# A graph network on one core: left-over edges between two parts of the scatters, nodes settled block by block, row parts split beside the first group

## What is computed

```python
h = relu(layernorm(x)) @ W                       # attention
score = h[src] @ a_src + h[dst] @ a_dst
e = exp(-leaky_relu(score)) * edge_weight
rowsum = segment_sum(e, src); h_prime = segment_sum(e * h[dst], src)
h_prime = where(rowsum == 0, h, h_prime) / where(rowsum == 0, 1, rowsum)
x = x + elu(h_prime)
...
y = relu(layernorm(x))                           # three layers
for i in range(3):
    aggr = segment_sum(relu(y[src] + edge_attr), dst)
    t = relu(bn((y + aggr) @ W1[i] + b1[i]))
    y = bn(t @ W2[i] + b2[i])                    # relu but for the last
out = x + y
```

## Time and profile before

| | us |
|---|---|
| median of 3 runs | 6582.67 |
| their range | 6578.78 to 6588.45 |
| the profiled execution | 6598.86 |
| its span, first to last instruction | 6597.1 |

### The profile page before, as it was taken

The page is one execution under the profiler, slowest core; times in us unless marked ns, Lnnn a source line. Parts: engine busy times, 40 slices in busy tenths (PEclk is TensorE's granted clock), DMA queues, the critical chain, the costliest instruction groups (busy, mean ns, idle before and its releaser), DMA issues.

```text
span 6597.1 us, 140067 instructions
## 1 busy us (share of the span) xinstructions
PE 4538.8 (69%) x50455; PEld 4306.8 (65%) x50456; DVE 3977.1 (60%) x7380; ACT 2704.7 (41%) x6857; POOL 3284.4 (50%) x2579
## 2 busy tenths in 40 slices
PE   1256561001018999999388888868888887888887
PEld 1256561000008999999388888858888876888886
DVE  6378781000005666666777777767777767777776
ACT  1398991000005777777333333343333334333333
POOL 0488887777770000000355665436666635656562
PEclk6576775555558999999699999989999998999998
DMA  9955543333323444453576777647777765777774
GB/s 169 265 170 166 185 136 137 115 111 112 109 92 121 150 150 150 150 150 127 152 224 223 224 227 223 211 150 227 235 232 232 233 188 181 229 226 226 225 232 134
DMA packets 664852, 1187.18 MB, mean 180 GB/s; under 512 B 151546, under 2 KB 489292, under 8 KB 664540
## 3 DMA queue, kind: packets, MB, share of 16 engines
q1 hardware_dynamic: 447020, 836.60, 40.4%
q10 hardware_dynamic: 135824, 178.67, 8.9%
q0 software_dynamic: 81696, 167.48, 8.3%
HBM read 967.99 MB, written 214.44 MB: 179 GB/s over the span
## 4 chain that ended last, share of the span: by engine, by line
PE 59%; issue 21%; DVE 10%; another core or an unknown queue 5%; SPq 3%; DMA 1%; ACT 1%; DVEq 1%; POOL 0%; POOLq 0%; ACTq 0%
PE ps L1569 18%; PE ps L1555 13%; PE ps L1488 10%; PE ps L1475 8%; PE ps L1579 4%; PE ps L1437 2%; PE ps L1438 2%; DVE dst_hot L1262 2%; PE ps L1427 2%; DVE sums L1270 1%; SPq L474 1%; DVE unit_attr L1289 1%; DVE field L1008 1%; PE ps L1613 1%
## 5 line engine op out<-in xcount | busy, mean ns | idle before, releaser
L665 POOL DMA_INDIRECT unit_x<-gin_rows,unit_src x1449 | 1854.8, 1280 | 1369.0 <-DVE unit_attr L1289 784.4
L1569 PE MATMUL ps<-dst_hot,sums 128*128 128x128 f32 x10584 | 1610.4, 292 | 175.8 <-issue 84.5
L632 POOL DMA_INDIRECT attr_by_slot<-abuf,ridx x1080 | 1397.7, 1294 | 514.9 <-issue 335.9
L836 ACT ACTIVATE sums<-sums 128x512 f32<-128x512 f32 x1512 | 837.6, 573 | 1842.1 <-DVE sums L1270 1370.9
L1569 PEld LDWEIGHTS ps<-dst_hot,sums 128*128 128x128 f32 x10584 | 1373.1, 199 | 233.5 <-issue 135.5
L1555 PE MATMUL ps<-x_parts,src_turned 128*128 128x128 bf16 x15876 | 1225.7, 225 | 230.2 <-issue 157.1
L1270 DVE TENSOR_TENSOR sums<-ps,sums 128x512 f32<-128x512 f32 x1512 | 911.5, 619 | 777.3 <-PE ps L1555 449.1
L1555 PEld LDWEIGHTS ps<-x_parts,src_turned 128*128 128x128 bf16 x15876 | 1074.8, 102 | 281.1 <-issue 259.9
L1475 PE MATMUL ps<-h_win,turned_hot 128*128 128x130 bf16 x7791 | 603.8, 221 | 446.1 <-issue 292.3
L1262 DVE TENSOR_TENSOR dst_hot<-iota_one,dl_slot 128x896 f32<-128x896 f32 x756 | 819.2, 1084 | 0.0
L1475 PEld LDWEIGHTS ps<-h_win,turned_hot 128*128 128x128 bf16 x7791 | 506.8, 97 | 467.6 <-issue 459.4
(11 more groups left out here) (229 smaller groups left out, 4743.4 us busy)
## 6 DMA issues: line engine op xcount, KB each, us to landing
sums<-attr_by_slot SPq DMA_DIRECT2D x756, 448.0 KB
src_turned<-rows_by_group SPq DMA_DIRECT2D x756, 224.0 KB
turned_hot<-rows_by_block ACTq DMA_DIRECT2D x392, 384.0 KB
attr_by_slot<-zeros SPq DMA_DIRECT2D x36, 3136.0 KB, 25.4
unit_attr<-in_edge_attr SPq DMA_DIRECT2D x204, 448.0 KB
abuf<-in_edge_attr SPq DMA_DIRECT2D x72, 960.0 KB
unit_x<-gin_rows,unit_src POOLq DMA_INDIRECT x1449
attr_by_slot<-abuf,ridx POOLq DMA_INDIRECT x1080
```

What stands on the lines that cost most here:

```text
L632: pool.indirect_dma_start(out=attr_table, out_offset=bass.IndirectOffsetOnAxis(ap=ridx[:, g, t0 + t:t0 + t + 1], axis=0), in_=abuf[:, k % ...
L665: pool.indirect_dma_start(out=unit_x[:, k % 2, t, :], out_offset=None, in_=gin_rows[n], in_offset=bass.IndirectOffsetOnAxis(ap=unit_src[:, ...
L836: act.activation(attr[:, first:first + tiles, :], attr[:, first:first + tiles, :], ACT.Relu).then_inc(s_msg, 1)
L1569: ins = pe.matmul(ps[:, 7, 0:WINDOW], attr[:, b, :], dst_hot[:, c % HOTS, b % G_TILES, :], start=(b == 0), stop=(b == BLOCKS - 1))
```

## The change

- **Scatters in two parts.** SyncE loads halves 2 to 33, then the left-over step's columns, then halves 34 to 71. GpSimd scatters 34 halves (510 transfers), gathers the left-over rows of attention, and scatters 38 halves (570). The left-over step takes one tile at a time instead of three (`STEP = 1`).
- **Attention in two loops.** Blocks 1 and 2 are a loop; then the sums of blocks 2 to 48 are cleared, the left-over step adds to them, and blocks 3 to 47 are a second loop, block 48 behind it. In the second loop a block's sums are added to what is there instead of copied.
- **Settling beside attention.** Block b - 3 is settled in the 9 chunks of block b, 11 VectorE instructions, one exp on ScalarE at chunk 5 and a load of the block's own rows there; the last three are settled behind attention. Normalisation goes in chunks of four blocks, even ones on ScalarE, odd ones on VectorE.
- **Row parts.** Only the first two chunks stand ahead of the layer's first gather; the others are formed beside the first group's halves, and the third part of every chunk on GpSimd (in `unit_x`, so the units begin two slots later, `LATE = 2`, and GpSimd's unit gathers wait for the seven subtractions). ScalarE's round 0 is written out and no longer in the loop.
- **A layer's left-over step** stands in the last round, ahead of half 11, with its own buffers and bank 6. SyncE loads for it behind half 17, GpSimd gathers behind unit slot 1. The next layer's first loads no longer wait for it.

Its core (lines left out at "..."):

```diff
-SPLIT_AT = CHUNKS // 2 * BY_CHUNK
-HALVES = ((0, SPLIT_AT), (SPLIT_AT, BLOCKS))
+TAIL_BLOCKS = 3
+SETTLE = 9
+PART_LEAD = 2
+ELU_AT = 5
+TAIL_FROM = BLOCKS - TAIL_BLOCKS
+OWN_LOADS = BLOCKS - TAIL_BLOCKS + 1
...
+LATE = 2
...
-STEP = 3
+FAR_LOADED = 16 * (6 + 1 + REST_U + 2 + T - 1 - TAIL_T)
+
+STEP = 1
+LEFT_AT = 3
+LOADS_THEN = 34
+LAST_LEFT = BY_UNIT + KEEP_AT + 1
...
-            for k in range(2, len(loads)):
+            for k in range(2, LOADS_THEN):
...
-            sp.wait_ge(s_kept, BLOCKS)
-            sp.dma_start(own[:, :, :], h_rows.rearrange("(b p) c -> p b c", p=P)).then_inc(s_out, 16)
-            store_rows(gin_rows[0], s_normed[1], 0, s_gin_row[0])
+            for k in range(LOADS_THEN, len(loads)):
+                load_half(k)
+            store_rows(gin_rows[0], lambda c: normed(sp, c), s_gin_row)
...
+                load_halves(n, ROUNDS - 1, 0, G_HALVES + 4)
                 load_left(((gidx[:, 0, :], left_src), (gidx[:, 1, :], left_dst), (gidx[:, 2, :], left_eid), (gsm[:, 0, :], left_v)),
                           s_lg[n]["loaded"], s_lg[n]["done"])
+                load_halves(n, ROUNDS - 1, G_HALVES + 4, R_HALVES)
                 if n + 1 < LAYERS:
 
-                    sp.wait_ge(s_summed, n + 1)
...
-            for k in range(len(loads)):
+            for k in range(LOADS_THEN):
...
-            pool.wait_ge(s_elu, 4)
+            for k in range(LOADS_THEN, len(loads)):
+                scatter_half(k)
+
             for n in range(LAYERS):
-                pool.wait_ge(s_gin_row[n], 16 * CHUNKS)
+                for c in range(G_CHUNKS):
+
+                    of = slice(c * G_TILES, (c + 1) * G_TILES)
+                    pool.wait_ge(s_part, 2 * (G_CHUNKS * n + c) + 2)
+                    pool.tensor_tensor(x_parts[:, 2, of, :], unit_x[:, c % 2, :, :], x_parts[:, 1, of, :], ALU.subtract).then_inc(s_last, 1)
+                pool.wait_ge(s_last, G_CHUNKS * (n + 1))
+                pool.wait_ge(s_gin_row, 16 * CHUNKS * (n + 1))
...
+                        if i == ROUNDS - 1 and k == 1:
+                            gather_left(((gx, gin_rows[n], gidx[:, 0, :]), (gy, edge_attr, gidx[:, 2, :])), s_lg[n]["loaded"], 4, s_lg[n]["gathered"])
...
-            with act.Fori(1, BLOCKS - 1) as b:
+            with act.Fori(1, LEFT_AT) as b:
                 for c in range(A_CHUNKS):
                     weigh(b, c, True)
-            for c in range(A_CHUNKS):
-                weigh(BLOCKS - 1, c, False)
...
+            def settle(p, more):
+                act.wait_ge(s_elu, p + 2)
+                act.activation(elu[:, 0, :], sums[:, p * SUM:p * SUM + D] if isinstance(p, int) else sums[:, bass.ds(p * SUM, D)], ACT.Exp).then_inc(s_expm, 1)
+                if more:
+                    load_own(p + 1)
+
+            act.wait_ge(s_elu, 1)
+            load_own(0)
+            with act.Fori(LEFT_AT, BLOCKS - 1) as b:
+                for c in range(A_CHUNKS):
+                    weigh(b, c, True)
+                    if c == ELU_AT:
+                        settle(b - LEFT_AT, True)
+            for c in range(A_CHUNKS):
+                weigh(BLOCKS - 1, c, False)
+                if c == ELU_AT:
+                    settle(BLOCKS - 1 - LEFT_AT, False)
+                    act.dma_start(own[:, :, :], h_rows[TAIL_FROM * P:COLS, 0:D].rearrange("(b p) c -> p b c", p=P)).then_inc(s_out, 16)
...
+                first_part(0)
+                for c in range(PART_LEAD):
+                    if n == 0:
+                        for t in range(c * CHUNKS // PART_LEAD, (c + 1) * CHUNKS // PART_LEAD):
+                            keep_columns(t)
+                    second_part(c)
+                    first_part(c + 1)
...
-                vec.tensor_copy(to, ps[:, 6, 0:SUM]).then_inc(s_kept, 1)
+                if onto:
+                    vec.tensor_tensor(to, to, ps[:, 6, 0:SUM], ALU.add).then_inc(s_kept, 1)
+                else:
+                    vec.tensor_copy(to, ps[:, 6, 0:SUM]).then_inc(s_kept, 1)
...
+                if c == 0:
+                    vec.wait_ge(s_kept, p + LEFT_AT)
+                    vec.tensor_scalar(col(stat[:, 0, :]), total, 0.0, None, ALU.is_equal).then_inc(s_settled, 1)
+                    vec.scalar_tensor_tensor(col(stat[:, 1, :]), total, 0.0, total, ALU.is_equal, ALU.add).then_inc(s_settled, 1)
+                elif c == 1:
+                    vec.wait_ge(s_settled, done + 2)
+                    vec.reciprocal(col(stat[:, 3, :]), col(stat[:, 1, :])).then_inc(s_settled, 1)
+                elif c == 2:
+                    vec.wait_ge(s_settled, done + 3)
+                    vec.scalar_tensor_tensor(col(stat[:, 2, :]), total, 0.0, col(stat[:, 3, :]), ALU.not_equal, ALU.mult).then_inc(s_settled, 1)
+                elif c == 3:
+                    vec.wait_ge(s_settled, done + 4)
+                    vec.tensor_scalar(rows, rows, col(stat[:, 2, :]), None, ALU.mult).then_inc(s_settled, 1)
...
+                    vec.scalar_tensor_tensor(rows, own[:, 0, :], col(stat[:, 0, :]), rows, ALU.mult, ALU.add).then_inc(s_elu, 1)
+                elif c == ELU_AT:
+                    vec.wait_ge(s_elu, p + 2)
+                    vec.scalar_tensor_tensor(node, rows, 0.0, node, ALU.max, ALU.add).then_inc(s_settled, 1)
+                elif c == 6:
+                    vec.wait_ge(s_expm, p + 1)
+                    vec.tensor_scalar(elu[:, 0, :], elu[:, 0, :], 1.0, -1.0, ALU.min, ALU.add).then_inc(s_settled, 1)
+                elif c == 7:
+                    vec.wait_ge(s_settled, done + 7)
+                    vec.tensor_tensor(node, node, elu[:, 0, :], ALU.add).then_inc(s_settled, 1)
+                else:
+                    one = slice(p, p + 1) if isinstance(p, int) else bass.ds(p, 1)
+                    vec.wait_ge(s_settled, done + 8)
+                    vec.bn_stats(ln[:, one, :].rearrange("p o s -> p (o s)"), node).then_inc(s_settled, 1)
...
-                        keep_block(b - 1)
+                        keep_block(b - 1, onto)
+                    if onto:
+                        settle(b - LEFT_AT, c)
...
-            with vec.Fori(1, BLOCKS - 1) as b:
+            with vec.Fori(1, LEFT_AT) as b:
                 block_of(b, True)
-            block_of(BLOCKS - 1, False)
-            keep_block(BLOCKS - 1)
+            link(vec.memset(sums[:, (LEFT_AT - 1) * SUM:BLOCKS * SUM], 0.0))
...
+            vec.sem_inc(s_elu, 1)
+            with vec.Fori(LEFT_AT, BLOCKS - 1) as b:
+                block_of(b, True, onto=True)
+            block_of(BLOCKS - 1, False, onto=True)
+            keep_block(BLOCKS - 1, True)
...
-                for c in range(G_CHUNKS):
-                    parts(c)
-                    last_parts(c)
-                vec.wait_ge(s_rest, 2 * G_CHUNKS * (n + 1))
+                    vec.wait_ge(s_part, 2 * G_CHUNKS * n + (1 if c == 0 else 2 * c + 1))
+                    if c >= 2:
+                        vec.wait_ge(s_last, G_CHUNKS * n + c - 1)
+                    vec.tensor_tensor(unit_x[:, c % 2, :, :], rows[:, of, :], x_parts[:, 0, of, :], ALU.subtract).then_inc(s_rest, 1)
...
+                        if last and h == LAST_LEFT:
+                            add_left()
...
+                            if first and c + PART_LEAD < G_CHUNKS:
+                                rest(c + PART_LEAD)
...
+                rest(0)
                 for c in range(TURN_LEAD):
                     turn_sources(0, c)
+                rest(1)
```

363 lines of the change are left out of this document (193 added, 170 removed).

## The result

Measured on one chip: the changed kernel 6613.23 us (median of 5), the kernel before 6578.78 us (median of 5). The ratio is 1.0045, 95% interval 1.0029 to 1.0061: slower by 0.45%, where 2.3% faster was forecast. (The ratio is that of the means, without one run of the changed kernel that took 6783 us in a slower state of the chip.) The profiled execution's span is 6611.5 us.

A forecast was written before the change was run, and what follows sets the result against it. Other engines were taken to get instructions slowly while GpSimd issues scatters back to back, then TensorE to be full in attention. Terms -24 + 14 - 73 - 26 - 43.5 = -152 us on 6597 gave 6430 us on the median, range 6200 to 6660.

The forecast's parts named there:

- The starved stretch: Attention beside GpSimd's second scatters: slow issue moves from block 0 into block 3; attention ends at 3108, -24 us.
- the size of the stock: Block 3's first pass: instructions TensorE already holds shorten it by 200 us, between 115 and 345.
- my 908: Block 3's first pass, starved: 9 chunks at 101 us each, 908 us before the stock is taken off.
- what they hold already runs at full pace: Attention beside scatters: only new instructions are slowed, so passes after block 3 take 23.3 us a block.
- rival B: Attention's second loop: repeated passes starve as well, attention ends at 3219, whole 6542 us; chance 0.12.
- Rival C: Attention: B, with scatters stretched to 1.6 us, ends at 3333; whole 6656 us; decides from about 1.5; chance 0.08.
- rival A: Attention beside scatters: no starving or it soon breaks off, whole 5750 to 5885 us; chance 0.18.
- Settling block by block: Attention's end to layer 0's first gather shrinks to 35 us, -73 with the first group; settling inside attention costs +14.
- Row parts: Ahead of layers 1 and 2's first gather: -13 us each, -26; GpSimd's subtractions take 1.1 to 4 us.
- The left-over step of a layer: End of each layer: 18.5 us becomes 4 (1 to 8) in the last round, -14.5 x 3 = -43.5 us.
- the first group: Start of each layer's rounds: five subtractions on VectorE beside the group lengthen it by 5.5 us.

The follow-up runs named there:

- e18: The kernel of e13, unchanged, on a chip where the kernel before takes some 6570 us: 6550.34 us, ratio 0.9939 to the kernel before.
- e11: Changed kernel with TensorE's code padded so that the three layers' rounds loops start at 210, 215 and 221 of 256: 5005.10 us, 0.9700 of the kernel before.
- e13: Changed kernel, 26 halves scattered first, the rest after block 3's sums, left-over columns loaded early, loops at 210, 215, 221: 4944.39 us, 0.9580 of the kernel before.
- e6: Changed kernel with a layer's left-over columns loaded at the start of the last round: 5168.16 us, 1.0019 of the kernel before.
- e7: TensorE's code moved by 168 places with 336 added fulfilled waits; its rounds' loops began at 31, 201 and 116; no whole time is given.
- e8: Changed kernel with TensorE's code padded so that the rounds' loops start at 185, 186 and 188 of 256: 5256.39 us, 1.0188 of the kernel before.
- e12: Kernel before with TensorE's code padded so that the rounds' loops start at 202, 203 and 204 of 256: 5144.33 us, 0.9967 of the kernel before unpadded.
- e1: The kernel before, unchanged, profiled again on another chip, where nothing starved: 5158.34 us.
- e5: The changed kernel, unchanged, on a chip where the kernel before takes about 5160 us: 5183.17 us, 1.0052 of the kernel before.
- e16: Kernel before with loops padded to start at 205, 210 and 215, on a chip of 6580: 6553.74 us, 0.9972 of the kernel before unpadded.
- e15: The kernel of e13 repeated on another chip that doesn't starve: 4953.29 us, 0.9583 of the kernel before.
- e17: The kernel of e13 repeated once more, on a further chip that doesn't starve: 4946.64 us, 0.9583 of the kernel before.

## Why the prediction was wrong

The measured 6613 us lies inside the range that I gave (6200 to 6660), but only because the rivals' times stretch it; the way, faster at 0.86, was wrong.

**The starved stretch: half right, two steps of it wrong.** Right were the start of block 3 (1354, forecast 1352), the end of the scatters (2118.5, forecast 2144 at 1.40 us each; they took 1.35), the 27 us behind them and the 100 us a chunk. Two steps failed. The first is the size of the stock: I took 200 us off the first pass, between 115 and 345, without a row that it was nearest to. In the changed kernel TensorE kept its pace for 5 us, 44 matmuls, hardly more than the 40 of the earlier trace rows:

```profile
1355.98 0.51 PE L1586 MATMUL ps<-h_win,turned_hot 128*128 128x130 bf16 x3 [3.10 <-issue]
...
1361.28 0.17 PE L1588 MATMUL ps<-s_parts,turned_hot 128*128 x1
1362.72 0.22 PE L1586 MATMUL ps<-h_win,turned_hot 128*128 128x130 bf16 x1 [1.27 <-issue]
```

From block 3's first chunk to its sums kept it took 793 us, 115 less than my 908 (some 12 of them since the ninth chunk has five tiles and not six): my lower bound, which would have given 2145, was the measured value. The second is "what they hold already runs at full pace": e18 shows passes two and three starved like the first. Either of the two, put right by itself, gives the measured end. With the smaller stock the first pass just fills the stretch; with a stock of 200 us and starved later passes, block 4 would have stood in the stretch from 2060 to 2145 and got less than one chunk done. So the changed kernel can't weigh them against each other; e18 shows that the second is wrong in any case. The time of attention's end thus came near rival B's, by which nothing of block 4 passes before the end (B's 3219 less the scatters' 26 us is 3193; measured 3189.8). Rival C wanted 1.5 us a scatter; it was 1.35.

The Trainium skill (Runtime: NRT & Kernel Launch, section Instruction fetch mechanics), that code is fetched ahead, "mostly hidden", was set against the forecast as rival A. The five packets in 900 us agree that fetching isn't what is slow there; A's conclusion, no starving, fell all the same on this chip, and held on four others. The Trainium skill's rule in the same section, that a taken branch out of the fetched code stalls, agrees with the pauses at each turn of the rounds' loop (4.44 us for "issue", 101 packets). It doesn't agree with the layers that keep their code: there the branch back over 1742 instructions brings none and shows no pause (e11, e13).

**Settling block by block: right.** The tail is 35.3 us (forecast 35). Its timeline, where the earlier trace rows have 114:

```profile
3189.81 0.29 DVE L1155 TENSOR_TENSOR sums<-sums,ps 128x129 f32<-128x129 f32 x1 [2.71 <-PE ps L1599]
...
3194.64 3.33 DVE L973 BATCH_NORM_AGGREGATE ln_mv<-ln 128x2 f32<-128x6 f32 x49
...
3225.18 2.40 PE L1669 MATMUL ps<-x_parts,src_turned 128*128 128x128 bf16 x21 [4.21 <-DVE src_turned L1358]
```

What moved into attention was forecast at 14 us and cost none: the last 45 blocks take (3189.8 - 2147.6) / 45 = 23.16 us each, as before ((3131.3 - 2091.1) / 45 = 23.12).

**Row parts: right, at the edge.** Products to the next gather shrank by 20.6 and 20.7 us (forecast 18.5). GpSimd's subtraction, which no row of before had:

```profile
L690 POOL TENSOR_TENSOR x_parts<-unit_x,x_parts 128x896 bf16<-128x896 f32 x21 | 42.1, 2006 | 1292.7 <-ACT x_parts L888 1292.7
```

2.0 us each, between the 1.1 and 4 of the prediction. With ScalarE's two copies ahead of it a chunk comes every 4.06 us, and the first group takes about 7 us more a layer (first gather to first window: 30.1 before, 37.2 after, on average) where 5.5 was said.

**The left-over step of a layer: the third step that failed.** The gain behind the last window is there (1.10 us of wait ahead of the products, forecast as good as none; 16.51 before):

```profile
5403.39 1.12 PE L1736 MATMUL ps<-agg,W_sb 128*128 128x512 f32 x2 [1.10 <-DVE agg L1382]
```

But I gave the step 4 us in its new place, since "its loads and gathers lie beside the halves". The loads stand in SyncE's line behind loads that wait for buffers, GpSimd waits for them, and VectorE, which has all other work of the round behind this step, waits for GpSimd: 14 to 16 us, outside the 1 to 8 that I allowed. Three times -14.5 became three times about -4; e6 shows that an earlier load gives some of it back.

**What no step named: the places of the code.** After these corrections the rounds should be 2 or 3 us longer in each layer; they are -9, +32 and +56. In layers 0, 1 and 2 TensorE's gaps over 1.8 us (without those of the row parts and the left-over step) sum to 40, 39 and 81 us after, against 11, 6 and 42 before, and the packets of code to 100, 74 and 101 against 56, 20 and 101. On chips of 5160, e7, e8, e11 and e12 show that such pauses follow the place of the code. On the chip of the result the place isn't all: the same programs brought code at some turns only (layer 0 of before, 56 packets where e1 has 101; layer 1 after, 74 where e5 has 101).

Of the 105 us by which the rounds missed the forecast, about 30 are the left-over step and about 5 the first group. The remaining 70 are settled only in part. The sums of gaps would cover them, but they don't fit layer 0 (29 us more of gaps, and yet shorter). And with the code held in both kernels on chips of 6580 a difference is left: the kernel before takes 3110 us for its three rounds (e16; 3161 without holding it), the changed one 3156 (e18, which has three edits more; 3240 in the changed kernel). Holding the code thus takes 51 and 84 us, 33 of the 79 by which the rounds differ, and 46 stay, on two chips where the kernel before differs by 26 us. A run of the changed kernel alone with held code on a chip of 6580 is missing, and so the cause of about half of the 70 stays open.

**The sum.** -152, +82 for attention's end (the stock, or the later passes), -14 for settling, +30 for the left-over step, about +70 for the rounds' rest (the places of the code are a part of it), +5 for the groups, less 7 for the shorter ends: +14. The spans differ by +14.4.

**The rivals.** A, no starving, is what chips of 5160 do, but even there its gain doesn't exist: without starving the kernel before has its scatters hidden already (e1), and the parted scatters only delay block 3, by 57 us. I had taken the starving for a property of the program, since I had the trace of one chip.

## What to carry to other kernels

A stretch in which every engine but one is slow for "issue" may belong to the chip (or its state), not to the kernel; run the kernel before on another chip before forecasting what a cure is worth. A step moved off the critical path takes its loads with it: ask where they stand in their own queue, and who is queued behind the wait. When an edit adds or removes instructions ahead of a long loop, compare the packets of kind "instruction" in the loop before and after, and shift the loop with a few idle instructions ahead of it: here that was worth 3.4% (e5 to e11), three times the edit itself.

## What the runs showed of the hardware that was not expected

- Two kinds of chip: beside back-to-back scatters (148 in 200 us in before and e1 alike), TensorE issues 2740 to 2750 matmuls in the 200 us from 1400 on four chips (e1, e5, e15, e17), and 71 to 77 on the others (changed kernel, e16, e18).
- Where it starves, it starves code that has been run before (e18), at 1.4 us an instruction (2.8 us for a matmul and its weight load), with 5 packets of code in 900 us. TensorE's stock at that moment lasts 5 us at full pace.
- On those chips also the layers' rounds, beside GpSimd's gathers, take 190 us more each with their code held (1033 to 1043 against 842 and 843).
- On chips of 5160 a loop of 1742 instructions of TensorE keeps its code or not by where it starts: kept at 202, 203, 210, 215 and 221 of 256 (and at 205, 210 and 215 on chip 15), brought again at 185 to 188 with two pauses a turn and, in one layer, at 204 with a long one. Where it is brought, a turn costs 4 to 9 us, a layer 40 to 90 us. The places are my count.
